# A graph layer's edge kernel: from a cycle of sixteen gathered groups and one picked group to eight and one, with each picked run's first product issued twice

## The reference

```python
h = jnp.maximum(_layernorm(x, axis=-1), 0.0)
x_i = h[dst]
x_j = h[src]
tmp = jnp.concatenate([x_i, x_j, edge_attr], axis=1)   # 48 + 48 + 32
h1 = jax.nn.relu(tmp @ W1 + b1)                        # hidden 128
msg = h1 @ W2 + b2                                     # 48
out = x + jax.ops.segment_sum(msg, dst, num_segments=12500)
```

## Time and profile before

| | |
|---|---|
| Median of the timed runs | 3817.3 us |
| The profiled execution | 3832.15 us |
| Its span, first to last instruction | 3830.3 us |
| Mean granted TensorE clock | 0.817 of full |
| PE busy | 3219.6 us, 84% |
| POOL busy | 2821.6 us, 74% |
| DVE busy | 2150.8 us, 56% |
| ACT busy | 1365.2 us, 36% |

### The profile page before, as it was taken

How to read it: one execution, slowest core, us unless ns; L and a number is a source line. 1 busy time by engine, 2 the same in 40 slices (tenths; PEclk the granted TensorE clock), 3 DMA queues, 4 the chain that set the end, 5 groups by cost and what they waited for, 6 DMA issues and landing times.

```text
span 3830.3 us, 77333 instructions
## 1 busy us (share of the span) xinstructions
PE 3219.6 (84%) x18440; PEld 2847.2 (74%) x18440; DVE 2150.8 (56%) x5362; ACT 1365.2 (36%) x4265; POOL 2821.6 (74%) x2968
## 2 busy tenths in 40 slices
PE   6888888888888888888888888888988888888887
PEld 6777777777777777777777777777777777777776
DVE  6555555555555555555555555555555555555553
ACT  5333333333333333333333333333333333333331
POOL 1677777777777777777777777777777777777776
PEclk9888878888788887878887888888788887888885
DMA  8533333333333333333333333333333333333334
GB/s 260 107 96 95 96 97 94 95 96 95 97 95 94 95 94 97 97 95 95 95 97 97 94 96 96 94 98 95 95 95 94 98 97 94 95 97 95 97 94 91
DMA packets 267909, 382.49 MB, mean 100 GB/s; under 512 B 87492, under 2 KB 150821, under 8 KB 266886
## 3 DMA queue, kind: packets, MB, share of 16 engines
q0 software_dynamic: 94464, 193.65, 20.1%
q1 hardware_dynamic: 173206, 186.79, 16.6%
HBM read 363.15 MB, written 16.94 MB: 99 GB/s over the span
## 4 chain that ended last, share of the span: by engine, by line
POOL 33%; issue 26%; PE 23%; DMA 7%; DVE 5%; ACT 4%; DVEq 2%; SPq 0%; POOLq 0%; ACTq 0%
POOL gath L416 33%; PE ps L956 8%; PE ps L972 8%; DMA gath<-b_table,idx 6%; PE ps L948 5%; DVE gath L719 2%; ACT gath L507 2%; DVEq L733 1%; PE ps L922 1%; DVE lhs L711 1%; ACT work L517 1%; DMA rhs<-a_table 1%; PE ps L962 0%; ACT idx L491 0%; DVE onehot L699 0%
## 5 line engine op out<-in xcount | busy, mean ns | idle before, releaser
L416 POOL DMA_INDIRECT gath<-b_table,idx x2952 | 2817.5, 954 | 989.0 <-issue 863.8
L956 PEld LDWEIGHTS ps<-onehot,gath 128*128 128x128 f32 x5904 | 878.1, 225 | 720.3 <-ACT gath L507 693.6
L956 PE MATMUL ps<-onehot,gath 128*128 128x48 f32 x5904 | 938.6, 310 | 560.3 <-ACT gath L507 556.4
L972 PE MATMUL ps<-h_tab,p_hot 128*128 128x480 f32 x3600 | 1115.1, 468 | 0.0
L948 PE MATMUL ps<-rhs,lhs 96*128 96x128 f32 x5904 | 1034.4, 330 | 24.0 <-DVE lhs L711 23.3
L507 ACT ACTIVATE gath<-gath 128x512 f32<-128x512 f32 x738 | 465.0, 630 | 1367.8 <-DVE gath L719 1363.5
L972 PEld LDWEIGHTS ps<-h_tab,p_hot 128*128 128x128 f32 x3600 | 838.9, 243 | 133.2
L948 PEld LDWEIGHTS ps<-rhs,lhs 96*128 96x128 f32 x5904 | 905.3, 234 | 24.4 <-issue 24.4
L719 DVE TENSOR_TENSOR gath<-ps,gath 128x512 f32<-128x512 f32 x738 | 510.1, 691 | 516.8 <-DMA gath<-b_table,idx 371.2
L711 DVE TENSOR_SCALAR_CACHE_REDUCE lhs<-nodes 48x512 f32<-48x512 f32 x738 | 549.1, 744 | 104.8 <-issue 61.0
L517 ACT ACTIVATE work<-ps,work 128x96 f32<-128x96 f32 x1800 | 453.9, 343 | 369.2 <-PE ps L972 364.5
(11 more groups left out here) (88 smaller groups left out, 935.2 us busy)
## 6 DMA issues: line engine op xcount, KB each, us to landing
nodes<-dst_row SPq DMA_DIRECT2D x783, 96.0 KB
lhs<-in_edge_t SPq DMA_DIRECT2D x738, 64.0 KB
gath<-b_table,idx POOLq DMA_INDIRECT x2952
rhs<-a_table SPq DMA_DIRECT2D x738, 24.0 KB
work<-key_row SPq DMA_DIRECT2D x45, 256.0 KB
b_table<-nodes SPq DMA_DIRECT2D x7, 512.0 KB, 3.3
a_table<-nodes SPq DMA_DIRECT2D x7, 512.0 KB, 5.2
work<-in_edge_t SPq DMA_DIRECT2D x90, 32.0 KB
```

The lines of the kernel that those rows point to most:

```text
L416: pool.indirect_dma_start(gath[:, u, t, :], None, b_table, bass.IndirectOffsetOnAxis(ap=idx[:, u, t:t + 1], axis=0)).then_inc(gathered[u], 16)
L956: mm = nc.tensor.matmul(ps_sum[:, k % 2 * WIN:(k % 2 + 1) * WIN], gath[:, u, t, :], onehot[:, u, t, :], start=(t == 0), stop=(t == TILES - 1))
L972: mm = nc.tensor.matmul(ps_run[:, r % 2, :].rearrange("p (j w) -> p j w", j=RUN_COLS), p_hot[:, t % 2, i, :], h_parts[:, first:first + BLO ...
```

## The change

`PERIOD` goes from 16 to 8, and the two groups ahead of the cycles (`LEAD`) and the padding group (`SPARE`) go. There are 782 groups in 87 cycles of eight gathered and one picked: 696 gathered and 86 picked. Every slot of a cycle now has a run, and the rest of the picked group's work moves to slots 3, 5 and 7. In `run_p` the loop starts at -1: the first product is issued with `stop=True`, and then again with `start=True`, which overwrites it, so that a run has 11 products. In the preamble SP loads the edges of the first four groups while the tables are still being stored, and `x_t` comes in one DMA that ACT issues, instead of two that SP issued.

```diff
-PERIOD = 16
-LEAD = 2
-SPARE = 1
+PERIOD = 8
+FILL = 1
...
-    cycles = (groups - LEAD + 1) // (PERIOD + 1)
+    cycles = (groups + 1) // (PERIOD + 1)
...
     @block.sync   (cycle)
                 for j in range(PERIOD):
-                    k = LEAD + c * PERIOD + j
+                    k = c * PERIOD + j
                     if k >= SLOTS:
                         load_edges(k, it, False)
                         load_a(k, it)
-                    if j == 12 and not final:
-                        load_p(c, it, first)
-                    if j == 14 and more:
+                    if j == 0 and not first:
+                        load_p(c - 1, it, c == 1)
+                    if j == PERIOD - 1 and more:
                         load_key(c + 1, it)
...
-            sp.dma_start(out_sb[:, win_at:n_nodes], x_t[:, win_at:n_nodes]).then_inc(xt_in, 16)
...
-            sp.dma_start(out_sb[:, 0:win_at], x_t[:, 0:win_at]).then_inc(xt_in, 16)
...
+            act.wait_ge(rel_ready, 1)
+            act.wait_ge(first_ready, 1)
+            act.dma_start(out_sb, x_t).then_inc(xt_in, 16)
...
     @block.scalar   (cycle)
-                    if j > 0 and j % 2 == 0 and not final:
-                        pick(j // 2 - 1, c, it)
-                    if j == 5 and not first:
+                    if j > 0 and not final:
+                        pick(j - 1, c, it)
+                    if j == 4 and not first:
                         keep_p_h(c - 1, it)
-                    if j == 8 and not first:
+                    if j == 6 and not first:
                         rectify_p(c - 1, it)
...
     @block.vector   (cycle)
-                    early = j == 9 and not first
+                    early = j == 7 and not first
                     if early:
                         add_out(k - 4, it)
                         copy_sums_p(c - 1, it)
                     if k >= 3:
                         add_z(k - 3, it)
...
+                    if j == 7 and more:
                         key_hot(0, c + 1, it)
                     if early:
                         add_out_p(c - 1, it, k - 4)
...
     @block.tensor
-                for i in range(BLOCKS):
+                for k in range(-FILL, BLOCKS):
+                    i = max(k, 0)
                     first = i + RUN_COLS * BLOCKS * q
                     mm = nc.tensor.matmul(
...
-                        start=(i == 0), stop=(i == BLOCKS - 1))
+                        start=(i == 0), stop=(k < 0 or k == BLOCKS - 1))
...
-                    k = LEAD + c * PERIOD + j
-                    if j == 9 and not first:
+                    k = c * PERIOD + j
+                    if j == 7 and not first:
                         make_sums_p(c - 1, it)
                         if not final:
-                            run_p(j // 2, c, it)
+                            run_p(j, c, it)
                         fold_p(c - 1, it)
                     if k >= 3:
                         make_sums(k - 3, it)
-                    make_z(k - 1, it)
-                    if j == 4 and not first:
+                    if j == 3 and not first:
                         turn_p(c - 1, it)
-                    if j == 6 and not first:
+                    if k >= 1:
+                        make_z(k - 1, it)
+                    if j == 5 and not first:
                         make_z_p(c - 1, it)
-                    if j % 2 and not final and (j != 9 or first):
-                        run_p(j // 2, c, it)
+                    if not final and (j != 7 or first):
+                        run_p(j, c, it)
                     if j % 2 == 0 and k >= 4:
                         fold(k - 3, it)
```

More of the change, by code:

```diff
@@ L55, in gnn @@
     late = 16
-    late_groups = late + 1
+    late_groups = late + 2
     front = n_nodes * 95 // 100
@@ L61, in gnn @@
     assert chunks * chunk_tiles == node_tiles and chunk_tiles == 2 * units
-    assert groups * e_cols == edge_cols and LEAD + cycles * (PERIOD + 1) == groups + 1 and cycles > 4
-    assert BLOCKS * PARTS >= node_tiles and RUN_COLS * split <= BANK and 2 * runs == PERIOD
-    assert PERIOD == 4 * SLOTS and LEAD == 2
+    assert groups * e_cols == edge_cols and cycles * (PERIOD + 1) == groups + 1 and cycles > 4
+    assert BLOCKS * PARTS >= node_tiles and RUN_COLS * split <= BANK and runs == PERIOD
+    assert PERIOD == 2 * SLOTS
     assert rounds * gen_cols * gen_k == n_nodes
@@ L281, in _ @@
                     sp.dma_start(key_row, key_sb[:, 2, :]).then_inc(key_stored, 16)
-            def load_edges(k, it, first):
-                s, g, u = it * PERIOD + k, group_of(k, it), k % SLOTS
-                if not first:
-                    sp.wait_ge(z_ready, s - SLOTS + 1)
-                sp.dma_start(dst_bc[:, u, :], dst_flat[:, ds(g * e_cols, e_cols)].partition_broadcast(WIN)
-                             ).then_inc(dst_loaded[u], 16)
-                sp.dma_start(lhs[e_row:k_rows, u, :], edge_t[:, ds(g * e_cols, e_cols)]).then_inc(loaded[u], 16)
+                    sp.wait_ge(dst_row_stored, 16)
+                    sp.wait_ge(ones_ready, 4)
+                    for k in range(SLOTS):
+                        load_edges(k, 0, True)
             def load_a(k, it):
@@ L338, in _ @@
                 load_a(k, 0)
-            for k in range(len(stores)):
-                sp.wait_ge(b_stored[k][0], 16 * ((chunks + 1) // 2))
-                sp.wait_ge(b_stored[k][1], 16 * (chunks // 2))
-            sp.dma_start(out_sb[:, 0:win_at], x_t[:, 0:win_at]).then_inc(xt_in, 16)
             cycle(0, 0, first=True)
-            with sp.Fori(0, cycles - 3) as it:
-                cycle(1, it)
+            cycle(1, 0)
+            with sp.Fori(0, cycles - 4) as it:
+                cycle(2, it)
             cycle(cycles - 2, 0, more=False)
@@ L816, in cycle @@
                         add_z(k - 3, it)
-                    if j == 1 and not first:
+                    if j == 0 and not first:
+                        sum_picked(2, c - 1, it)
+                    if j == 1 and not final:
+                        key_hot(1, c, it)
+                    if j == 2 and not first:
                         sum_picked(3, c - 1, it)
-                    if j == 2 and not first:
                         dst_hot_t_p(c - 1, it)
                     if j == 3 and not final:
-                        key_hot(1, c, it)
+                        key_hot(2, c, it)
+                    if j == 4 and not final:
+                        sum_picked(0, c, it)
                     if j == 4 and not first:
@@ L825, in cycle @@
                     if j == 5 and not final:
-                        sum_picked(0, c, it)
-                    if j == 7 and not final:
-                        key_hot(2, c, it)
-                    if j == 9 and not final:
+                        key_hot(3, c, it)
+                    if j == 6 and not final:
                         sum_picked(1, c, it)
-                    if j == 11 and not final:
-                        key_hot(3, c, it)
-                    if j == 13 and not final:
-                        sum_picked(2, c, it)
-                    if j == 15 and more:
+                    if j == 7 and more:
                         key_hot(0, c + 1, it)
@@ L848, in cycle @@
                         part_masks(c, it)
-            for k in range(LEAD):
-                make_hot(k, 0)
-                make_hot_t(k, 0)
             key_hot(0, 0, 0)
@@ L862, in _ @@
                 if k % 2:
-                    add_out(k - 4, 0)
+                    add_out(k - 4, 0, items - 1)
                 else:
```

45 lines of the change are left out of this document (23 added, 22 removed).

## The result

The changed kernel takes 3919.8 us, median of 4 runs (3919.3 to 3922.4), against 3820.1 us for the kernel before on the same chip (4 runs, 3816.1 to 3823.3). The ratio is 1.0263, with a 95% interval of 1.0245 to 1.0281: 2.6% slower. The forecast was 3930 us.

The account below looks back on a forecast made before the run. PE was taken to bound the kernel, with 40.3 + 1.8 + 2.1 = 44.2 us a cycle. 82 + 44 + 3757 + 61 and 2 outside the span made 3946, against the median 3930 us; range 3745 to 4015.

Parts of the forecast that it names:

- PE's work in a cycle: All PE steps of a new cycle at full clock, added up: 40.3 us, equal to POOL's 40.3, so no slack.
- The repeated product: First product issued twice in each of a cycle's eight runs on PE: 8 x 0.236 = 1.9 us a cycle.
- The rival of the free product: Repeated product on PE costs nothing: 1.9 us a cycle less, 42.3, against the median 3770 us; chance 0.03.
- The wait at the cycle's end: PE idles before the next group's sums, for a chain through DVE and ACT that begins at `fold_p`: 1.8 us a cycle.
- The clock behind it: PE's clock halves behind the idle stretch at the cycle's end, slowing sums, z and run: 2.1 us a cycle.
- the lower case: Clock falls only once PE has resumed, sparing one of sums, z and run: some 1.6 us a cycle.
- the upper one: Clock falls in PE's idle stretch and returns in the middle of the run: 2.6 us a cycle.
- The first rival: PE's clock holds or comes back at once behind the gap: cycle 42.1, 3753 us, 1.7% faster; chance 0.13.
- PE sets the pace: PE, not POOL, bounds the new cycle; POOL waits for ACT's index copy some 330 us in all.
- DVE's stall goes: The 3.06 us stall before `add_z` where DVE's loop turns should vanish with the shorter loop; chance that it stays 0.08.
- The start: First gather at 81.9 us, then some 44 us until PE enters cycle 1; nothing taken for the preamble's loads.
- a loss of the whole run at half clock: Behind the cycle-end gap sums, z and all eleven products pass at half clock: 3.6 us a cycle.

Follow-up runs that it names:

- e1b: Changed kernel without the repeated first product of each run (ten products, not eleven): 3670.8 us, ratio 0.9605 to the kernel before.
- e6: Kernel before with only the repeated product added to each run: 3818.4 us, ratio 0.9998.
- e10: Changed kernel with run 0 split around slot 0's sums and z (seven products ahead, three behind) and no repeated product: 3640.3 us, ratio 0.9529.
- e5: Changed kernel with DVE's hardware loop holding two cycles instead of one, same compute instructions: 4015.7 us, ratio 1.0513 to the kernel before.
- e2b: Changed kernel with seven unused products filling PE's gap between z of slot 7 and the sums of slot 0: 3686.8 us, ratio 0.9653.
- e3b: Changed kernel with all of run 0 moved ahead of slot 0's sums, nothing added: 3789.8 us, ratio 0.9922 to the kernel before.
- e11: e9 with x_t's load moved from ACT to SP, behind SP's first loads of a_table: 3631.7 us, ratio 0.9509 to the kernel before.
- run 0: Not a kernel: the first of a cycle's eight runs of products on PE, eleven products, in the changed kernel behind slot 0's z.
- e9: Changed kernel with run 0 split, seven products ahead of slot 0's sums and four behind its z; part masks a slot later: 3635.3 us, ratio 0.9516.
- e1: Changed kernel without the repeated product, run on another chip where the kernel before took 4940.3 us: 5200.8 us, ratio 1.0523.

## Why the prediction was right, step by step

The sum was 82 + 44 + 3757 + 61 + 2 = 3946, brought to 3930. The trace has 83.6 + 53.7 + 3720 + 60.1 = 3917.4 and 2 outside the span; the 85 cycles go from 137.3 to 3857.3 us, the ends of `make_z` of slot 7, and have 43.76 on the mean (43.79 by `fold_p`'s products). Its parts:

- *PE's work in a cycle.* Taken as 40.3 us. Measured 43.79 - 1.60 - 2.81 = 39.38. e1b's undisturbed cycle gives the same by another way: 37.60 of work and eight products of 0.235 make 39.48. The term that was 1 us too large is the sum of single steps: I took each step from one place and added it eight times. In the trace a run followed by sums is over in 2.50, not 2.60, and the sums behind a run in 0.82, not 0.93; `turn_p` and `make_z_p` were 0.3 us too high together.
- *The repeated product* was taken at its full price, 1.9 us a cycle. In a cycle that PE bounds its own time is 1.8, and removing it gave 2.84, since the clock gave back 1.0 (e1b). Where POOL bounds the cycle it is nothing (e6, e10): the product takes its time in every kernel and is paid for only where PE bounds the cycle. The rival of the free product failed because PE does so here.
- *The wait at the cycle's end.* Taken 1.8, measured 1.60, in every cycle. The chain through DVE was the one described: e5 made DVE's part of it 2.33 longer and PE's wait 2.30.
- *The clock behind it.* Taken 2.1, with half of the cycles spared one step. Measured 2.81 (e2b). The mechanism was right, and the clock fell in every one of the 84 cycles; the fall was the longer one in 69. Against e2b's cycle of 40.98 a long fall costs 3.1 us and a short one 1.6, so the lower case was right in size, the upper one (2.6) too small, and it should have had most of the weight. The first rival, that the clock holds, is what e2b made true: 3686.8. The sum gave it 3753, with a cycle of 42.1; e2b's is 40.98, for the work that I took too large. The Trainium skill (TensorE: Matmul & The Clock Gate, "Why this matters for your kernels") warns only of longer gaps; waits of 1.60 us here and of 1.08 us in e3b had the clock fall behind them.
- *PE sets the pace.* POOL's waits for indices were to be 330 us; they are 376.5.
- *DVE's stall goes.* It did, and e5 shows that the length of the loop's body decides (207 records in the trace without a stall, 349 and some 410 with one), since the work and its order were left as they are. The price was read as 3.06; inside the chain it was 2.33. The Trainium skill (Runtime: NRT & Kernel Launch, "Instruction fetch mechanics") says that a taken branch whose target is outside the two pages at hand waits for a fetch; the packets of the queue agree with that. By the 256 instructions that the Trainium skill gives such a page, an estimate puts 349 records into two pages as well as 207, so its figures alone don't tell which loop stalls.
- *The start.* Taken 44 us from the first gather to cycle 1, measured 53.7. This is the term that was wrong: I wrote that the preamble's loads change some microseconds either way, and put nothing. x_t is now one DMA of 2343.8 KB, issued at 84.98; the load of `a_table` issued right behind it landed 21.5 us later, and PE began its z at 108.20 instead of 100.36. (In the kernel before a first part of x_t, 1344 KB, stood ahead of that load too.) POOL stood 16.43 us for want of buffers:

```profile
119.90 0.94 POOL L407 DMA_INDIRECT gath<-b_table,idx  x1 [16.43 <-ACT idx L488]
```

When this order alone is changed, little of it comes back (e11): 3.6 us by the medians, 1.5 by the first `fold_p`.

So the near hit is in part errors against each other. In the cycle, work 0.9 and wait 0.2 too high against the clock 0.7 too low left 44.2 for 43.76: 37 us too much over 85 cycles. At the two ends 10 us too little. And the execution profiled this time stood at the median of its runs (3919.28 and 3919.76), while I had taken off 0.39%, 15 us, for that of before. Without this deduction the forecast would have been 3946; that it came within 10 us is partly luck. One sum is wrong in the text itself: a loss of the whole run at half clock makes a cycle of 45.7 us by its own terms, and so some 4060 us, not the 4015 that it gives as the end of the range from the first rival to that loss.

## What to carry to other kernels

When an engine that only had waits to fill becomes the bound, every small thing that was free is paid in each round: here a product issued twice went from 0.0% to more than 6%. Ask not what a step costs but what it costs with the new bound, and test parts of a change apart and together. If TensorE waits in front of a step at each turn of a loop, put work of its own into that wait, and leave some for the next step that waits: all of run 0 there opened a gap one slot later, and a split of it left 0.22 and 0.39 us of waiting, behind which the clock held.

## What was not expected of the hardware

- Waits of 1.08 and 1.60 us were followed by half clock in most cycles (72 of 84 in e3b; 84 of 84 in the changed kernel and 78 of 84 in e1b), waits of 0.22 and 0.39 us in e9 in none. But the length alone doesn't decide: of e10's 33 waits of 1.1 to 2.0 us in the whole cycles only 11 were followed by it, and in the kernel before a wait of 1.56 us (ahead of the sums at 2018.43) was not.
- Behind the same wait of 1.60 us the clock was at half for some 7 us in most cycles of one kernel, and for half of that in most of another that issues one product less in each run. What decides it stays open.
- Products with no use cost less than idling: seven of them in the gap made the cycle 2.81 us shorter.
- On one chip the kernel before took 29% more time, and the four kernels traced there had pauses of about a microsecond in PE's stream without a wait (the kernel before wasn't traced there). Ratios measured there didn't carry over (e1 was 1.0523 there and 0.9605 elsewhere).
